# A graph layer on one core: fourteen superblocks of 128 sorted lists and 1344 gathered tiles, in place of fifteen superblocks of 125 lists and 1250 gathered tiles

## The chip, the core and the metric

The kernel runs on one core of a Trainium2 chip. The metric is the device time of one execution in microseconds (us); lower is better. The engines are named as in the profile: PE is TensorE, with its weight loads apart as PEld, DVE is VectorE, ACT is ScalarE, POOL is GpSimd, and SP is SyncE, which here only issues DMAs.

## The reference

There are 12500 nodes with 16 features and 400000 edges. The edges come sorted by their destination `dst`; `src` is random. Each edge has 64 attributes and one weight.

```python
h = jnp.maximum(_layernorm(x, axis=-1), 0.0)
# _L0_gnn_ref(h, edge_attr_64, edge_weight1, src, dst, W_node, W_review):
h = feat @ W_node.T
rf = review_feat @ W_review.T
m = (h[src_idx] + rf) * edge_w
rst = jax.ops.segment_sum(m, dst_idx, num_segments=N_NODES)
# the result
x = x + rst
```

The two projections are linear, so the kernel first sums raw attributes and raw `h` rows by destination, into `acc` (64 + 16 rows, and 16 more for a low half of `h`, by 12500 columns), and multiplies by the weights once at the end.

## The kernel before

**Tiles.** 128 edges make a tile, 3125 in all. A few tiles with neighbouring destinations are a group. For a group a 0/1 matrix is made per tile, of 128 edges by a window of 64 nodes that begins at the group's lowest destination (`find_hits`, L770, on DVE); ACT multiplies it by the edge weights (`weigh`, L551); PE multiplies the tile's 128 edges of values by it and sums over the group in one PSUM region (`sum_p` L1045, `sum_s` L1054); DVE adds the region to `acc` (`add_p` L791, `add_s` L799). A group has five tiles.

**Two ways to get `h[src]`.** For the first 1250 tiles (250 groups, "p") POOL gathers the rows from HBM, one indirect DMA for each tile (L493). For the other 1875 tiles (15 superblocks of 125 tiles, 375 groups, "s") the rows come from a table of `h` in SBUF, which holds an upper and a lower f16 half. The edges of a superblock are taken as 125 lists of 128, and each list is sorted by `src` before the main loop. Rank `j` of all lists then lies within a few chunks of 128 nodes, so `look_up` (L1019) finds it by matmuls: a 0/1 matrix `hot` of 128x125 (made on DVE, L707) times a run of table chunks. The ranks are handled in 16 steps of 8. A step has 8 ranks, 4 low digits and 2 halves, that is 64 matmuls, each with `WIDTH[x]` times 16 moving columns. DVE picks the right chunk with a mask (L749, L756, L763, L767). After 16 steps `turn_ranks` (L1027) transposes, ACT and DVE split the result into two f16 halves (L570, L808), and `unsort` (L1033) brings the rows back to the order of the edges with a permutation matrix `perm` from DVE (L781), one matmul for each tile. ACT copies them beside the attributes (`place_h`, L564).

**Phases.** Superblock 0 is looked up in a first phase (16 steps, each with one p group). Then a hardware loop of 14 phases looks up superblock t+1 while it unsorts and sums superblock t. In step x of a phase PE does, in this order, `look_up(t + 1, x)`, the `unsort` of the groups of step x+1, one `sum_p`, and the `sum_s` of the groups of step x. 25 groups go over the steps 1 to 15 by the list `SUMS`, so a step has one or two. A tail unsorts and sums the last superblock and the last 10 p groups. It also checks whether any list fell outside `WIDTH` (L917, L920); the number of passes over everything is 1 when none did and the reach of every group fits in the window.

**Order.** All is written out by hand; each engine runs its own list and waits on semaphores. Buffers: `RP = 8` slots for gathered groups, `RS = 5` for sorted ones, 4 for each of the selection matrices.

## Time and profile before

| | |
|---|---|
| median of 3 runs | 2637.76 us (2636.53 to 2643.74) |
| the profiled execution | 2632.39 us, its span 2630.7 us |
| until the first `look_up` | 160.4 us |
| first phase | 130.4 us |
| the 14 phases of the loop | 2232.5 us, 159.5 us each |
| tail, until the last add | 89.9 us |
| product with the weights, output | 17.5 us |

Times in the rows are microseconds unless marked ns, counted from the first instruction. "PEclk" is the granted share of TensorE's clock: 1.00 is 2.4 GHz and 0.50 is 1.2 GHz. "issue" marks idle time for which the profile names no other engine. PE pipelines its matmuls, so the time of a run of matmuls is best read from the start of one row to the start of the next.

### The profile page before, as it was taken

The page shows a single profiled execution, that of the slowest core. Times are in us where ns is not written, and L with a number is a line of the kernel's source. Part 1 is how long each engine was busy: PE and PEld are TensorE (multiplying, and loading weights), DVE is VectorE, ACT ScalarE, POOL GpSimd, SP SyncE. Part 2 cuts the span into 40 slices and gives each one's busy share as a digit, 9 for nine tenths or more (in the row PEclk, how much of TensorE's full clock was granted, in tenths as well). Part 3 has the DMA queues.
Part 4 walks back from the last instruction along what each step waited for, and adds up shares of the span by engine and source line. Part 5 has one row for each costly group of instructions (what it writes and reads, how often), then busy time and mean ns, then how long its engine had stood idle before and what let it go on. Part 6 is the DMA issues. An engine that isn't in the chain of part 4 may idle for free.

```text
span 2630.7 us, 72159 instructions
## 1 busy us (share of the span) xinstructions
PE 1966.3 (75%) x23874; PEld 1832.1 (70%) x23874; DVE 1524.6 (58%) x3239; ACT 911.5 (35%) x3561; POOL 1448.9 (55%) x1301
## 2 busy tenths in 40 slices
PE   1047788787878878787887878878788887887766
PEld 1046677777777777777776777777677777777765
DVE  6944555655555556555665656555555565656554
ACT  2011342433333333333433324333333333334343
POOL 3636665565655656556565555655556565656630
PEclk9577787787877878778887878878778787878855
DMA  3322233333323333233243323333333333333342
GB/s 112 48 60 57 63 77 70 80 75 68 82 68 72 77 74 77 65 84 78 65 90 68 78 62 84 83 67 74 68 69 85 67 81 74 77 70 79 75 64 43
DMA packets 512156, 191.30 MB, mean 73 GB/s; under 512 B 472234, under 2 KB 495359, under 8 KB 511479
## 3 DMA queue, kind: packets, MB, share of 16 engines
q1 hardware_dynamic: 469361, 173.64, 27.7%
q0 software_dynamic: 40000, 10.32, 4.1%
q8 instruction: 223, 3.65, 0.6%
q10 hardware_dynamic: 2368, 2.02, 0.3%
q14 instruction: 204, 1.67, 0.2%
HBM read 182.96 MB, written 2.89 MB: 71 GB/s over the span
## 4 chain that ended last, share of the span: by engine, by line
PE 65%; issue 22%; DVE 7%; ACT 2%; DMA 2%; another core or an unknown queue 1%; DVEq 1%; ACTq 0%; SPq 0%
PE found L1019 35%; PE seg L1054 16%; PE seg L1045 8%; PE edge_h L1033 5%; DMA big<-in_dst_dram 1%; ACT mid L551 1%; PE found L1027 1%; DVE by_rank L658 1%; DVE big L658 1%; DVE big L659 1%; DVE by_rank L659 1%; DVE perm L781 1%; DVE big L707 1%; ACT by_rank L570 1%
## 5 line engine op out<-in xcount | busy, mean ns | idle before, releaser
L493 POOL DMA_INDIRECT vals_p<-h_ext,idx_t x1250 | 1433.8, 1147 | 1094.9 <-PE seg L1045 700.6
L1019 PE MATMUL found<-table,big 128*128 128x128 f16 (+4 forms) x15360 | 1070.7, 233 | 377.5 <-issue 328.2
L1019 PEld LDWEIGHTS found<-table,big 128*128 128x128 f16 x15360 | 958.9, 111 | 473.5 <-issue 470.1
L551 ACT ACTIVATE sel_p<-hit_p,wgt_t 128x64 f32<-128x64 f16 x1250 | 325.4, 335 | 1208.6 <-issue 703.7
L1054 PE MATMUL seg<-mid 128*96 128x64 f32 x3750 | 506.0, 310 | 48.9 <-ACT mid L564 33.8
L1054 PEld LDWEIGHTS seg<-mid 128*96 128x96 f32 x3750 | 485.2, 224 | 52.0 <-issue 42.9
L551 ACT ACTIVATE mid<-mid,wgt_t 128x64 f32<-128x64 f16 x1875 | 468.2, 333 | 15.2 <-DVE mid L770 14.5
L749 DVE TENSOR_TENSOR masked<-found,mask 125x512 f32<-125x512 f32 x240 | 165.4, 689 | 518.5 <-PE found L1019 332.5
L707 DVE TENSOR_SCALAR big<-low_all,own 128x2004 f16<-128x2004 f16 x484 | 336.6, 738 | 11.8 <-DMA low_all<-low_dram 11.8
L1045 PE MATMUL seg<-sel_p,vals_p 128*80 128x64 f32 x2500 | 303.3, 282 | 36.0 <-issue 35.2
L1045 PEld LDWEIGHTS seg<-sel_p,vals_p 128*80 128x80 f32 x2500 | 272.5, 194 | 47.0 <-issue 45.2
L791 DVE SCALAR_TENSOR_TENSOR acc<-seg,count_p,acc 80x64 f32 x250 | 69.8, 279 | 336.5 <-issue 334.6
L1033 PE MATMUL edge_h<-by_rank,perm 128*128 128x32 f16 x1875 | 169.5, 241 | 65.9 <-issue 46.4
L781 DVE TENSOR_TENSOR perm<-edge_no,pos_t 128x768 f16<-128x768 f16 x375 | 193.4, 547 | 0.0
L1033 PEld LDWEIGHTS edge_h<-by_rank,perm 128*128 128x128 f16 x1875 | 132.7, 130 | 80.9 <-issue 67.7
L770 DVE TENSOR_TENSOR mid<-iota,rel_t 128x320 f16<-128x320 f32 x375 | 168.3, 480 | 0.0
L799 DVE SCALAR_TENSOR_TENSOR acc<-seg,count_s,acc 96x64 f32 x375 | 104.5, 279 | 107.8 <-issue 87.5
L564 ACT COPY mid<-edge_h 128x160 f32<-128x160 f32 x375 | 92.1, 287 | 215.4 <-PE edge_h L1033 184.7
L756 DVE COPY_PREDICATED masked<-mask,found 125x512 f32<-125x512 uint8 (+3 forms) x225 | 138.3, 615 | 39.0 <-DVE masked L749 33.8
L770 DVE TENSOR_TENSOR hit_p<-iota,rel_t 128x320 f16<-128x320 f32 x250 | 119.5, 478 | 0.0
L763 DVE TENSOR_TENSOR masked<-masked 125x256 f32<-125x256 f32 x240 | 100.6, 419 | 0.5
L570 ACT CAST by_rank<-found 128x1000 f16<-128x1000 f32 x30 | 29.8, 992 | 121.4 <-issue 58.0
(129 smaller groups left out, 440.3 us busy)
## 6 DMA issues: line engine op xcount, KB each, us to landing
low_all<-low_dram SPq DMA_DIRECT2D x120, 501.0 KB
mid<-in_edge_attr_dram SPq DMA_DIRECT2D x375, 160.0 KB
vals_p<-in_edge_attr_dram SPq DMA_DIRECT2D x250, 160.0 KB
vals_p<-h_ext,idx_t POOLq DMA_INDIRECT x1250
big<-in_src_dram SPq DMA_DIRECT2D x1, 1562.5 KB
big<-in_dst_dram SPq DMA_DIRECT2D x1, 1562.5 KB
big<-in_edge_weight_dram SPq DMA_DIRECT2D x1, 1562.5 KB
h_ext<-mid SPq DMA_DIRECT2D x2, 781.2 KB
```

The costliest lines, as they stand in the source:

```text
L493: pool.indirect_dma_start(vals_p[:, q % RP, j, R:F], None, h_ext, bass.IndirectOffsetOnAxis(ap=idx_t[:, q * J + j:q * J + j + 1], axis=0), ...
L551: last = nc.scalar.activation(sel[:, j, :], hit[:, j, :], ACT.Copy, scale=wgt_t[:, bass.ds(tile + j, 1)])
L707: return nc.vector.tensor_scalar(hot[:, k, a, :], low_all[:, k, :], own[:, a:a + 1], None, ALU.is_equal)
L749: nc.vector.tensor_tensor(masked[:], rows_of(x, 0, FOLD), masks_of(x, 0, FOLD), ALU.mult).then_inc(masked_low, 1)
L756: nc.vector.copy_predicated(masked[:, :, 0:WIDTH[x] - FOLD, :], masks_of(x, FOLD, WIDTH[x]), rows_of(x, FOLD, WIDTH[x])).then_inc(masked_i ...
L770: return nc.vector.tensor_tensor(hit, iota[:, 0:WINDOW].unsqueeze(1).to_broadcast([P, J, WINDOW]), rel_t[:, bass.ds(tile, J)].unsqueeze(2) ...
L781: nc.vector.tensor_tensor(perm[:, g % RS], edge_no[:], pos_t[:, bass.ds(u, 1), g, :].to_broadcast([P, P, J + 1]), ALU.is_equal).then_inc(p ...
L799: nc.vector.scalar_tensor_tensor(out=window, in0=seg_s(g), scalar=count_s[0:FS, 0:1], in1=window, op0=ALU.mult, op1=ALU.add).then_inc(acc_ ...
L1019: last = nc.tensor.matmul(found[x % 2][:, r * P:r * P + n], hot[:, x // 2 % 2, a, col:col + P], rows, start=(a == 0 and part == 0), stop=( ...
L1033: last = nc.tensor.matmul(edge_of(g)[:, q * 2 * H:(q + 1) * 2 * H], perm[:, g % RS, :, q], by_rank[:, :, :, g * J + q].rearrange("p i f -> ...
L1045: last = nc.tensor.matmul(seg_p(x), vals_p[:, slot, j, :], sel_p[:, x % RH, j, :], start=(j == 0), stop=(j == J - 1))
L1054: last = nc.tensor.matmul(seg_s(g), vals_s[:, g % RS, j, :], sel_s[:, g % RS, j, :], start=(j == 0), stop=(j == J - 1))
```

## The change

The lists become 128 for each superblock in place of 125, and the superblocks 14 in place of 15. The sorted edges are now the first 1792 tiles, and the gathered ones the last 1344 (11 tiles of the two sets overlap; their entries in the gathered set are switched off by a destination of -1). A sorted group has 8 tiles, a gathered one 6, and every step of a phase has exactly one of each, so `SUMS` is gone. The window is 56 nodes wide. `WIDTH` and `BACK`, which say how many chunks a step looks through and from where, have new values; the sum of the sixteen widths goes from 112 to 105. `find_hits` now works in f16, with the tiles innermost, so ACT reads `hit[:, :, j]` with a step of 6 or 8 elements where it read 64 in a row. The hit matrices have 2 slots in place of 4 or 5, and DVE waits for ACT before it writes one again; `RP` goes from 8 to 4, `RS` from 5 to 4. The last phase is taken out of the hardware loop and written out, without p hits for a later one; the tail has no p groups.

```diff
-J = 5
-WINDOW = 64
-LISTS = 125
-GATHERED = 10
-SORTED = 15
-GROUPS = LISTS // J
+WINDOW = 56
+LISTS = P
+SORTED = 14
+GROUPS = 16
+JS = LISTS // GROUPS
+JP = 6
-WIDTH = (4, 6, 7, 7, 7, 8, 8, 8, 8, 8, 8, 8, 7, 7, 6, 5)
+WIDTH = (4, 5, 6, 7, 7, 7, 8, 8, 8, 7, 8, 8, 7, 6, 5, 4)
-HOT = COLS * LISTS + 4
+HOT = COLS * LISTS
-RS = 5
-RP = 8
+RS = 4
+RP = 4
+RM = 2
-SUMS = [[]] + [list(range(25 * (x - 1) // 15, 25 * x // 15)) for x in range(1, STEPS)]
...
-        edge_no = sb("edge_no", [P, P, J + 1], F16)
+        edge_no = sb("edge_no", [P, P, JS], F16)
...
-                    for j in range(J):
+                    for j in range(JP):
                         pool.indirect_dma_start(
...
+            nc.scalar.copy(rel_half[:], rel_t[:]).then_inc(rel_halved, 1)
...
-                        last = nc.scalar.activation(sel[:, j, :], hit[:, j, :], ACT.Copy, scale=wgt_t[:, bass.ds(tile + j, 1)])
+                        last = nc.scalar.activation(sel[:, j, :], hit[:, :, j], ACT.Copy, scale=wgt_t[:, bass.ds(tile + j, 1)])
...
-                def find_hits(hit, tile):
-                    return nc.vector.tensor_tensor(hit, iota[:, 0:WINDOW].unsqueeze(1).to_broadcast([P, J, WINDOW]),
-                                                   rel_t[:, bass.ds(tile, J)].unsqueeze(2).to_broadcast([P, J, WINDOW]), ALU.is_equal)
+                def find_hits(hit, tiles, tile):
+                    return nc.vector.tensor_tensor(hit, edge_no[:, 0:WINDOW, 0:tiles],
+                                                   rel_half[:, bass.ds(tile, tiles)].unsqueeze(1).to_broadcast([P, WINDOW, tiles]), ALU.is_equal)
+                def hits_p(u, x, first=False):
+                    if not first:
+                        dve.wait_ge(sel_p_in, ps * NQ + u * STEPS + (x - RM + 1))
+                    find_hits(hit_p[:, x % RM], JP, u * (STEPS * JP) + (SORTED_TILES + x * JP)).then_inc(hit_p_in, 1)
...
                         if step:
+                            fold_four(u, x)
+                            dve.wait_ge(summed_s, ps * NSG + t * GROUPS + x + 1)
+                            dve.sem_inc(begun_dve, 1)
+                            add_p(u, x, added_t + 2 * x)
+                            fold_two(u, x)
+                        if step + 1 < STEPS:
+                            make_perm(t, step + 1)
...
+                        after(nc.vector.tensor_copy(rel_half[:], rel_t[:]))
...
                         look_up(t + 1, step)
                         if step == 0:
                             pe.wait_ge(rank_in, ps * (2 * SORTED) + t * 2 + 2)
-                        for g in groups_unsorted(step):
-                            unsort(t, g)
-                        bank_free(added_t, step, False)
-                        sum_p((t + 1) * STEPS + step, t * 2 + 2 + step // RP, step)
-                        for g in SUMS[step]:
-                            sum_s(t, g)
+                            unsort(t, 0)
+                        if step + 1 < STEPS:
+                            unsort(t, step + 1)
+
+                        if step >= 2:
+                            pe.wait_ge(acc_step, added + 2 * (step - 1))
+                        sum_p(t + 1, step)
+                        sum_s(t, step)
                     turn_ranks(t + 1)
+
+                with pe.Fori(0, SORTED - 2) as t:
+                    phase(t, pe.snap(ps * NG + t * PER_PHASE + (STEPS + 1)))
+                phase(SORTED - 2, ps * NG + ((SORTED - 2) * PER_PHASE + STEPS + 1))
```

On PE, the first rows of a phase in the loop, before: step 0 has one `unsort` of five tiles and no sum of sorted tiles, and step 1 has two. `found0` and `found1` are the two banks of `look_up`, `edge_h` those of `unsort`, and `seg` with `mid` is `sum_s`.

```order
L1019 MATMUL found0<-table,big 128x64 x64
L1080 REGISTER_ALU
L1031 ISA
L1033 MATMUL edge_h0<-by_rank,perm 128x32 x5
L1038 ISA
L1042 ISA
L1043 ISA
L1045 MATMUL seg0<-sel_p,vals_p 80x64 x5
L1019 MATMUL found1<-table,big 128x96 x64
```

The same place on PE with the change:

```order
L1025 MATMUL found0<-table,big 128x64 x64
L1079 REGISTER_ALU
L1037 ISA
L1039 MATMUL edge_h0<-by_rank,perm 128x32 x8
L1037 REGISTER_ALU
L1039 MATMUL edge_h1<-by_rank,perm 128x32 x8
L1044 ISA
L1047 ISA
L1048 REGISTER_ALU
L1050 MATMUL seg0<-sel_p,vals_p 80x56 x6
L1056 ISA
L1059 MATMUL seg0<-mid 96x56 x8
```

The `unsort` of two groups, and the first `sum_s`, now stand in step 0, ahead of the second `look_up`.

On DVE, the first rows of a phase in the loop, before; `mask` is made first, then half of a `hot` block (`big`), two `perm` and the hits of three groups (`hit_p`, `mid`):

```order
L732 TENSOR_TENSOR mask<-digit_now,digit 125x1024
L723 ISA
L707 TENSOR_SCALAR big<-low_all,own 128x2004 x2
L781 ISA
L781 TENSOR_TENSOR perm<-edge_no,pos_t 128x768
```

The same place on DVE with the change:

```order
L741 TENSOR_TENSOR mask<-digit_now,digit 128x1024
L732 ISA
L716 TENSOR_SCALAR big<-low_all,own 128x2048 x2
L795 ISA
L795 TENSOR_TENSOR perm<-edge_no,pos_t 128x1024
L786 ISA
L779 ISA
L779 TENSOR_TENSOR hit_p<-edge_no,rel_half 128x336
```

There is now one `perm`, of eight tiles; it is the one of group 1, which PE's second `unsort` of step 0 takes.

## Rows read from the trace of the kernel before

**Rows 1.** The page: busy time, share of the span, instructions of each engine
```profile
PE 1966.3 (75%) x23874; PEld 1832.1 (70%) x23874; DVE 1524.6 (58%) x3239; ACT 911.5 (35%) x3561; POOL 1448.9 (55%) x1301
```

**Rows 2.** Stages: length; busy of PE, PEld, DVE, ACT, POOL; PEclk, DMA share, GB/s
```profile
160.39:290.77 130.38, 93.55 (x1201) 82.84 (x1201) 63.25 (x133) 26.48 (x97) 77.45 (x75) 0.81 0.26 58
290.77:2523.26 2232.49, 1780.17 (x22050) 1668.31 (x22051) 1285.83 (x2872) 815.64 (x3248) 1291.08 (x1126) 0.81 0.33 74
2523.26:2613.20 89.94, 65.24 (x477) 62.72 (x477) 46.44 (x111) 43.85 (x185) 15.73 (x10) 0.50 0.32 49
```

**Rows 3.** Groups of PE in the loop (290.77 to 2523.26): busy, mean ns, idle before
```profile
L1054 PE MATMUL seg<-mid 128*96 128x64 f32 x3500 | 462.9, 305 | 31.6 <-ACT mid L564 17.2 <-issue 14.2
L1033 PE MATMUL edge_h<-by_rank,perm 128*128 128x32 f16 x1750 | 158.6, 240 | 54.3 <-issue 46.4 <-DVE perm L781 5.4 <-DVE by_rank L808 2.1
L1019 PE MATMUL found<-table,big 128*128 128x64 f16 x896 | 39.3, 210 | 36.6 <-DVE by_rank L808 27.0 <-issue 9.3
```

**Rows 4.** Timeline of PE at full clock, two stretches
```profile
2204.85 2.23 PE L1019 MATMUL found<-table,big 128*128 128x64 f16 x64 [1.42 <-DVE by_rank L808]
...
2481.91 0.90 PE L1045 MATMUL seg<-sel_p,vals_p 128*80 128x64 f32 x10
2482.64 1.86 PE L1054 MATMUL seg<-mid 128*96 128x64 f32 x20
2484.34 2.87 PE L1019 MATMUL found<-table,big 128*128 128x112 f16 x55
2487.41 0.26 PE L1019 MATMUL found<-table,big 128*128 128x112 f16 x2 [0.20 <-issue]
2488.19 0.21 PE L1019 MATMUL found<-table,big 128*128 128x112 f16 x1 [0.52 <-issue]
```

**Rows 5.** Timeline of PE at half clock: first phase, and the tail
```profile
160.39 3.59 PE L1019 MATMUL found<-table,big 128*128 128x64 f16 x64 [18.44 <-DVE table L813]
163.80 1.58 PE L1045 MATMUL seg<-sel_p,vals_p 128*80 128x64 f32 x10
...
173.39 5.48 PE L1019 MATMUL found<-table,big 128*128 128x112 f16 x57 [1.07 <-issue]
...
2591.22 3.43 PE L1054 MATMUL seg<-mid 128*96 128x64 f32 x20 [2.41 <-ACT mid L564]
2594.44 0.50 PE L1033 MATMUL edge_h<-by_rank,perm 128*128 128x32 f16 x5
2594.76 3.43 PE L1054 MATMUL seg<-mid 128*96 128x64 f32 x20
```

**Rows 6.** Clock of stretches within rows 4 and 5: PE busy (x), PEclk, DMA share, GB/s
```profile
2482.70:2484.40 1.70, 1.70 (x24) 1.00 0.06 11
...
173.50:178.80 5.30, 5.30 (x58) 0.50 0.17 34
```

**Rows 7.** Queues of one phase (1250 to 1410): packets, MB, share
```profile
q8 instruction: 16, 0.26, 0.7%
```

**Rows 8.** Groups of DVE and ACT in the loop, as in rows 3
```profile
L781 DVE TENSOR_TENSOR perm<-edge_no,pos_t 128x768 f16<-128x768 f16 x351 | 181.1, 547 | 0.0
L770 DVE TENSOR_TENSOR mid<-iota,rel_t 128x320 f16<-128x320 f32 x350 | 157.1, 480 | 0.0
L551 ACT ACTIVATE mid<-mid,wgt_t 128x64 f32<-128x64 f16 x1750 | 437.0, 332 | 0.7
```

**Rows 9.** Group of POOL over the span, as in rows 3
```profile
L493 POOL DMA_INDIRECT vals_p<-h_ext,idx_t x1250 | 1433.8, 1147 | 1094.9 <-PE seg L1045 700.6 <-issue 313.8 <-ACT rel_t L511 41.0
```

**Rows 10.** Timeline of PE, and of DVE, at the start of a phase
```profile
1254.28 1.59 PE L1045 MATMUL seg<-sel_p,vals_p 128*80 128x64 f32 x10
...
1256.61 1.52 DVE L707 TENSOR_SCALAR big<-low_all,own 128x2004 f16<-128x2004 f16 x2
1258.05 1.01 DVE L781 TENSOR_TENSOR perm<-edge_no,pos_t 128x768 f16<-128x768 f16 x2
```

**Rows 11.** A group of DVE in the prologue, as in rows 3
```profile
L658 DVE TENSOR_TENSOR by_rank<-big 125x960 f32<-125x960 f32 x14 | 16.9, 1207 | 0.5
```

More of the change, by code:

```diff
@@ L56 @@
 COLS = 2 * RANKS
-HOT = COLS * LISTS + 4
+HOT = COLS * LISTS
 SCALE = 8192.0
 ROUNDER = float(3 << 22)
-RS = 5
-RP = 8
+RS = 4
+RP = 4
 RH = 4
-SUMS = [[]] + [list(range(25 * (x - 1) // 15, 25 * x // 15)) for x in range(1, STEPS)]
-REST = GATHERED * GROUPS - SORTED * STEPS
-PER_PHASE = STEPS + GROUPS
-def step_of(g):
-    return [y for y in range(STEPS) if g in SUMS[y]][0]
-def place_p(x, last):
-    return min(x, REST if last else x) + sum(len(SUMS[y]) for y in range(x))
-def place_s(g, last):
-    x = step_of(g)
-    return min(x + 1, REST if last else x + 1) + g
+RM = 2
+PER_PHASE = 2 * STEPS
 def bass_gnn_preln(
@@ L389, in _ @@
                              h_ext[bass.ds(roll * (SHIFT * P), NPAD), :].rearrange("(k p) f -> p k f", p=P)).then_inc(h_back, 16)
-                for q in range(RP):
-                    load_p(q, q)
+                for step in range(RP):
+                    load_p(0, step)
                 for g in range(RS):
@@ new lines, in phase @@
+                            fold_two(u, x)
+                        if step + 1 < STEPS:
+                            make_perm(t, step + 1)
+                        else:
+                            make_perm(t + 1, 0)
+                        if step:
+                            add_s(t, x, added_t + 2 * x + 1)
+                        if step + 2 < STEPS:
+                            hits_p(u, step + 2)
+                            hits_s(t, step + 2)
+                        else:
+                            if not last:
+                                hits_p(u + 1, step + 2 - STEPS)
+                            hits_s(t + 1, step + 2 - STEPS)
@@ L976, in turn_blocks @@
                 for q, tile in enumerate(tiles):
[L977 removed]
+                    rows = tile.shape[0]
+                    last = nc.tensor.transpose(turn_bank[n % 4][:, q * rows:(q + 1) * rows], tile, ident[0:rows, 0:rows])
                 last.then_inc(turned, 1)
[L980 removed]
+            pe.wait_ge(src_float, 2)
             for k, m in idx_parts:
[L982 removed]
+                turn_blocks([src_g[:, (k + q) * P:(k + q + 1) * P] for q in range(m)])
             pe.wait_ge(rel_done, 1)
@@ L1052, in sum_s @@
                     pe.wait_ge(h_placed, ps * NSG + u * GROUPS + g + 1)
-                    for j in range(J):
+                    for j in range(JS):
                         last = nc.tensor.matmul(seg_s(g), vals_s[:, g % RS, j, :], sel_s[:, g % RS, j, :],
-                                                start=(j == 0), stop=(j == J - 1))
+                                                start=(j == 0), stop=(j == JS - 1))
                     last.then_inc(summed_s, 1)
-                def bank_free(before, x, last):
-                    if x >= 2:
-                        added = (place_s(SUMS[x - 2][-1], last) if SUMS[x - 2] else place_p(x - 2, last)) + 1
-                        pe.wait_ge(acc_step, before + added)
                 pe.wait_ge(pass_open, ps + 1)
@@ L1069, in _, with phase @@
                         pe.wait_ge(acc_step, ps * NG + (1 + step - 1))
-                    sum_p(step, step // RP, step)
+                    sum_p(0, step)
                 turn_ranks(0)
-                with pe.Fori(0, SORTED - 1) as t:
-                    added_t = pe.snap(ps * NG + t * PER_PHASE + (STEPS + 1))
+                def phase(t, added):
                     for step in range(STEPS):
```

473 lines of the change are left out of this document (232 added, 241 removed).

## The prediction

> **What bounds the kernel now.** I read the page's busy times first. PE is busy for 75% of the span, DVE 58%, POOL 55%, ACT 35% [rows 1]; no engine is full, so the shares alone decide nothing. Then the stages. The loop of 14 phases is 2232.5 of the 2630.7 us, 159.5 us a phase. In it PE is busy for 1780.2 us, the next engines for 1291.1 (POOL) and 1285.8 (DVE), and the granted clock is 0.81, so PE runs at full clock for some 60% of the time and at half clock for the rest [rows 2]. PE is idle for 2232.5 - 1780.2 = 452 us of the loop, 32.3 a phase. In the groups of PE, the waits that name another engine are 17.2 (ACT's `place_h`), 27.0 and 2.1 (the split of the ranks) and 5.4 (`perm`), together 51.7 us or 3.7 a phase. The rest, 28.6 us a phase, is "issue" [rows 3]. The timeline shows what that is: in the midst of one `look_up`, whose matmuls wait for nothing new, PE stops for about 0.5 us again and again, with one or two matmuls between the stops [rows 4]. The instruction queue q8 moves 16 packets in a phase [rows 7], and a phase has 1575 matmuls, so one packet goes with 98 of them; 28.6 / 16 = 1.8 us of stop to a packet. I read this as PE running out of instructions. So a phase is the time of PE's own matmuls, plus a toll that goes with their number, plus little else. What matters is how many phases there are, and what a phase costs PE.
>
> **What a matmul costs.** The granted clock of a stretch says which level a row belongs to [rows 6]. `look_up` by the length of its rows, half clock: 64 of 64 columns in 3.59 us, 56 ns each; 57 of 112 columns in 5.48 us, 96 ns [rows 5]. That is 13.3 ns for each unit of `WIDTH` (16 columns). Full clock: 64 of 64 columns in 2.23 us, 35 ns; 55 of 112 columns in 2.87 us, 52 ns [rows 4], 5.8 ns a unit. So `look_up` pays for its columns. The others from the start of one row to the start of the next. `sum_p` (two records a tile): 10 in 0.73 us at full clock, where the row itself is 0.90 long; at half clock the row is 1.58, so about 1.4. `sum_s`: 20 in 1.70 and in 3.22 us. `unsort`: 5 in 0.32 us, 64 ns each, at half clock [rows 4, 5]. The sums cost 73 and 85 ns a record with 80 and 96 weight columns over the same 64 moving columns, a ratio like 80 to 96 (140 and 161 at half clock). They pay for weight columns, so I give the window of 56 nothing on PE.
>
> **The change on PE, for one phase.** `look_up`: 7 units fewer, 64 matmuls each, 448 x 5.8 = -2.6 us at full clock, -6.0 at half. `sum_p`: 96 tiles for 80, 32 records more: +2.3, +4.4. `sum_s`: 128 tiles for 125, 6 more: +0.5, +1.0. `unsort`: 3 more: +0.2. Together +0.4 at full clock and -0.4 at half: nothing. The matmuls go from 1575 to 1616, so the toll grows by 2.6% of 28.6: +0.7 us. Bounds: 0, if the smaller number of waits (32 groups unsorted and summed for 50) saves as many instructions, and +1.8, one packet more.
>
> *The start of a phase.* Two `unsort`s now stand in step 0, and the second wants `perm` of group 1, which DVE makes after `mask` and half a `hot` block. In the trace DVE's `hot` pair of step 0 ends at 1258.1 [rows 10]; one wider `perm` (0.55 us for 768, some 0.7 for 1024 [rows 8]) makes 1258.8. PE was free at 1254.3 and did `sum_p` and `look_up` of step 1 before it needed a new `perm`. Now three more matmuls of the first `unsort` take it to 1254.5, and it waits some 4.3 us in step 0. Against this stand `sum_s` of group 0, which no longer waits for `place_h` later (17.2 + 5.4 us named in the loop, 1.6 a phase), and the instructions that can arrive meanwhile. Between 0 and +4.3 I take +1.
>
> *The weights of `unsort`* are read with a step of 8 elements where it was 6, since `perm` holds 8 tiles side by side. No row shows step 8. At the lower bound the cost stays 64 ns a matmul; `look_up`, with weights in a row and twice the moving columns, takes 56 ns at half clock [rows 5], so the step does seem to cost something. For the upper bound I take double, 64 x 128 = +8.2 us a phase. The nearest row is `unsort` itself, so 0. The Trainium skill, "SBUF — State Buffer", section "Door 1: The DMA port swizzle", says that SBUF has lines of 16 bytes and that each access which goes to a new line pays. By that rule steps of 6 elements (12 bytes) touch a new line three times in four and steps of 8 every time, 64 x 4/3 = 85 ns, and the whole time would be some 38 us above mine (an estimate; the 64 ns against 56 agrees in direction).
>
> Phase: 159.5 + 0 + 0.7 + 1 + 0 = 161.2 us. There are 13: 2096 us.
>
> **The other engines in a phase.** DVE drops from 41 hit matrices of 0.48 us to 32. They are all f16 now, as `perm` is, and 768 elements of that take 547 ns where 320 with an f32 input take 480 [rows 8]; so about 0.3 to 0.4 us each, 11 us for 20. `perm` 11 for 14, nine adds fewer. DVE gets about 10% lighter and was not the bound: a gain of 0 in the loop. ACT: 224 activations for 205 at 250 ns (437.0 / 1750 [rows 8]) is 56 of 161 us. Even at double the cost for the step in its input ACT stays under PE, at 112. DVE's new waits for ACT are for work of two steps ago: nothing. POOL: busy time and issue gaps make (1433.8 + 313.8) / 1250 = 1.40 us a gather [rows 9], 8.4 a step for six, against 161.2 / 16 = 10.1. With four slots a gather group is asked for three steps, 30 us, before its sum. Hidden; without that cover each step would be POOL's 8.4 us or more.
>
> **First phase.** 130.4 us [rows 2], the same for the mix of clocks. PE: `look_up` -2.6 or -6.0, `sum_p` +2.3 or +4.4: -0.3 to -1.6, I take 129.8. A step is 8.1 us there, less than POOL's 8.4, but four groups are ready and the 12 others end 12 x 8.4 = 101 us after the first sum (at about 165), before PE is at the last step (282). Hidden.
>
> **Prologue.** 160.4 us. On the path is DVE: 56 min/max operations of 960 elements, one group of 14 at 1.2 us [rows 11], now 896 elements; at 1.1 ns an element, about 70 ns less each, -3.9 us. Nine operations over all keys lose 128 elements each, -1.2. Against it four operations over `dst` grow from 3200 to 3584 elements, +1.7, and `edge_no` +0.3. Makes 157.3. ACT's `rel_half` cast falls into its wait for the sort.
>
> **Tail.** 89.9 us at half clock [rows 2]. Now 16 even steps without `sum_p`: 16 x 161 + 8 x 64 ns = 3.1 us of PE, 49.5 in all. ACT needs 8 x 0.25 us [rows 8] and a copy of some 0.4, 2.4 a step, and stays behind PE. PE was idle for 89.9 - 65.2 = 24.7 us of the tail [rows 2]: waits for `place_h` in steps with two groups (2.41 us in one [rows 5]), which go, and DVE's check of the lists and its bookkeeping for a next pass, which stay. I take half, 12.5: 62 us. With all of it the tail is 74, at full clock near 50.
>
> **Sum.** 157.3 + 129.8 + 2096 + 62 + 17.5 = 2462.6 us of span, 168 under 2630.7. The profiled execution took 1.7 more than its span, so 2464.3; the median of the runs shown was 2637.76 / 2632.39 = 1.002 of it. **2469 us**.
>
> **Rivals.**
> - *Phases get shorter too (0.17).* The even steps and the lighter DVE take away the 3.7 us of named waits, and the stops fall where PE waits anyway. For it: PE still waits for others at the start of phases. Against: 28.6 of 32.3 us are not such waits. At 154 us a phase: 2469 - 13 x 7 = 2378.
> - *The step of 8 costs PE (0.14).* If the cost goes with the length of the step, 64 x 8 / 6 = 85 ns, 14 x 2.7 us, 2507; at double, 14 x 8.2 us, 2584. For it, the slow `unsort` rows; against, that nothing here shows the weights, and not a fixed cost, to make them slow. The page named above would have the lower of the two.
> - *POOL becomes the bound (0.05).* It does from 161 / 96 = 1.68 us a gather on, against 1.40 now; at 1.75 the phase is 168 us, 2469 + 13 x 6.8 = 2557. For it, the smaller ring and more f16 operations on DVE; against, 20% of room.
> - *Slower than before (0.04).* The granted clock. By the costs above the matmuls of a phase take 97 us at full clock and 172 at half (112 units at 5.8 or 13.3 ns with 12 or 3 ns on top of each `look_up` matmul, the sums and `unsort` as above, 2 or 3 us for `turn_ranks`). The 127.2 us now (1780.2 / 14) mean that 40% of this work is done at half clock. If the new wait of 4 us at each start keeps the clock low afterwards, so that 60% is, a phase gains 15 us and stands at 176: 2469 + 13 x 15 = 2664. From 57% on it is slower. Against: PE stops in each phase now, and the clock came back each time.
> - *The change needs more than one pass (under 0.01).* Worked out from the drawn inputs, the widest group reaches 51 nodes in a window of 56 and no list falls outside the new `WIDTH`; so one pass. Two would be near 4900 us.
>
> **Range.** The forecast has 0.60; its own terms (a phase of 158 to 164, tail 50 to 75) give 2416 to 2518. With the lower half of the second rival and the upper half of the first the range is **2390 to 2550**. 0.3% is about what a measurement of this kernel can tell from no change, so: faster 0.95, within it 0.01, slower 0.04.
>
> **What would show it.** 13 phases of 159 to 163 us; PE idle about 32 us in each, most of it issue, in bursts about 100 matmuls apart; `unsort` matmuls 64 ns apart; a wait of PE for `perm` of about 4 us in step 0 of each phase; hit matrices of 0.3 to 0.4 us; POOL gathers waiting for `sum_p`; a tail near 62 us. It is wrong if the clock in the loop is off 0.81 by more than 0.03, if the idle time of PE in a phase is not tied to the number of matmuls, or if the gathers end a wait of PE.

## The result, and the profile after

The changed kernel takes 3094.4 us (median of 4 runs, 3092.8 to 3100.2), the kernel before 2637.2 us on the same chip. The ratio is 1.173, 95% interval 1.171 to 1.176: 17% slower, where 2469 us and a gain of 6% were predicted. The profiled execution took 3092.84 us, its span is 3090.9.

The stages, with the columns of [rows 2]: prologue up to 155.60, then the first phase, the twelve looped phases, the last phase (written out behind the loop), and the tail.
```profile
155.60:298.20 142.60, 90.81 (x1064) 78.78 (x1063) 54.09 (x120) 29.61 (x102) 85.17 (x87) 0.76 0.23 53
298.20:2822.00 2523.80, 1905.02 (x19393) 1813.54 (x19393) 960.47 (x2124) 844.68 (x2904) 1107.40 (x1155) 0.65 0.27 60
2822.00:2996.60 174.60, 141.25 (x1616) 134.39 (x1616) 78.39 (x177) 68.34 (x231) 73.65 (x73) 0.72 0.30 68
2996.60:3081.40 84.80, 60.72 (x442) 52.76 (x442) 37.75 (x78) 37.53 (x128) 0.00 (x0) 0.52 0.25 46
```
A looped phase lasts 2523.8 / 12 = 210.3 us, where 161.2 was predicted and 159.5 is the value of before. Its 50.8 us more have two parts. PE is idle for (2523.8 - 1905.0) / 12 = 51.6 us of it, 32.3 before: 19.3 us. PE's busy time is 158.8 us, 127.2 before: 31.6 us. The matmuls themselves did not grow, since at one clock level each costs what it did (`sum_s` 16 in 2.56 us at half clock, from 1385.89 to 1388.45 below, 160 ns each, 161 before); it is the level. With the prediction's 97 us at full and 172 at half clock, 158.8 means (158.8 - 97) / 75 = 82% of the work at half clock, 40% before. The granted clock is 0.65 where it was 0.81.

The page's busy times, and the groups of PE and POOL over the span (busy, mean ns of one, idle before them and what ended it):
```profile
PE 2226.8 (72%) x22779; PEld 2105.2 (68%) x22779; DVE 1250.6 (40%) x2627; ACT 1014.7 (33%) x3421; POOL 1327.9 (43%) x1394
...
L487 POOL DMA_INDIRECT vals_p<-h_ext,idx_t x1344 | 1314.7, 978 | 1641.8 <-PE seg L1050 1252.3
L1025 PE MATMUL found<-table,big 128*128 128x112 f16 (+4 forms) x14336 | 1196.0, 259 | 676.6 <-issue 657.7
```
The same group of `look_up` in the kernel before, over its span:
```profile
L1019 PE MATMUL found<-table,big 128*128 128x128 f16 (+4 forms) x15360 | 1070.7, 233 | 377.5 <-issue 328.2 <-DVE by_rank L808 27.0 <-DVE table L813 18.4
```
Inside the look-ups the idle time that no wait explains has doubled, 328.2 to 657.7 us, over fewer matmuls. POOL, which makes the gathers, has slack: it waits 1252.3 us for `sum_p` to free a buffer.

Where in a step this happens is seen in PE's timeline, and in POOL's of the same stretch:
```profile
1384.27 1.83 PE L1050 MATMUL seg<-sel_p,vals_p 128*80 128x56 f32 x12
1385.89 2.77 PE L1059 MATMUL seg<-mid 128*96 128x56 f32 x16
1388.45 4.00 PE L1025 MATMUL found<-table,big 128*128 128x112 f16 x46
1392.66 0.21 PE L1025 MATMUL found<-table,big 128*128 128x112 f16 x1 [0.21 <-issue]
1394.08 0.21 PE L1025 MATMUL found<-table,big 128*128 128x112 f16 x1 [1.21 <-issue]
1395.50 1.65 PE L1025 MATMUL found<-table,big 128*128 128x112 f16 x16 [1.21 <-issue]
1396.95 0.67 PE L1039 MATMUL edge_h<-by_rank,perm 128*128 128x32 f16 x8
1397.44 1.82 PE L1050 MATMUL seg<-sel_p,vals_p 128*80 128x56 f32 x12
```
```profile
1386.91 0.94 POOL L487 DMA_INDIRECT vals_p<-h_ext,idx_t  x1 [5.80 <-PE seg L1050]
...
1391.92 0.94 POOL L487 DMA_INDIRECT vals_p<-h_ext,idx_t  x1 [0.30 <-issue]
1393.17 0.94 POOL L487 DMA_INDIRECT vals_p<-h_ext,idx_t  x1 [0.30 <-issue]
1400.07 0.99 POOL L487 DMA_INDIRECT vals_p<-h_ext,idx_t  x1 [5.96 <-PE seg L1050]
```
Nearly every step is like this one. The end of `sum_p` frees a buffer, POOL makes the six gathers for it one behind another, from 1386.9 to 1394.1, and by the fifth PE stops in the look-up, comes back for one matmul, stops again for 1.2 us, and runs on at 1395.5, 1.4 us after the last gather has ended. The windows show the clock of this cycle (columns as in the stages):
```profile
1384.00:1391.00 7.00, 7.00 (x64) 7.00 (x62) 4.04 (x9) 0.37 (x1) 3.18 (x4) 0.50 0.47 114
1393.00:1395.00 2.00, 0.21 (x1) 0.19 (x2) 0.00 (x0) 2.00 (x8) 0.94 (x1) 1.00 0.09 8
1396.00:1401.00 5.00, 5.00 (x46) 5.00 (x43) 2.91 (x5) 0.37 (x1) 0.93 (x1) 0.50 0.07 17
```
In this step full clock is granted while PE stands still, half clock (1.2 GHz) when it works again.

The written-out last phase shows the rest. Its last four steps have no gathers to make for later ones: POOL's last begins at 2969.4. PE's timeline there:
```profile
2971.33 0.55 PE L1039 MATMUL edge_h<-by_rank,perm 128*128 128x32 f16 x6 [0.51 <-issue]
2971.83 1.60 PE L1050 MATMUL seg<-sel_p,vals_p 128*80 128x56 f32 x12
...
2975.79 4.38 PE L1025 MATMUL found<-table,big 128*128 128x96 f16 x64
2980.00 0.66 PE L1039 MATMUL edge_h<-by_rank,perm 128*128 128x32 f16 x8
2980.48 1.04 PE L1050 MATMUL seg<-sel_p,vals_p 128*80 128x56 f32 x12
2981.36 1.52 PE L1059 MATMUL seg<-mid 128*96 128x56 f32 x16
2982.72 2.46 PE L1025 MATMUL found<-table,big 128*128 128x80 f16 x64
2985.01 0.66 PE L1039 MATMUL edge_h<-by_rank,perm 128*128 128x32 f16 x8
```
The last stop of this kind is at 2971. The look-ups behind it run through all 64 matmuls, and from `sum_p` at 2980.5 to the end of the phase they do so at full clock. The step shown takes 2985.01 - 2980.00 = 5.0 us, where a looped one takes 13.2 on average; it is one of the narrow ones (80 columns for 64 to 128), so only a part of that is the stop and the clock.

### The profile page after: what moved, and what is told of

Same layout as the page of the kernel before. It is cut to its first block, busy times and chain, and to the rows that moved or that the text cites. A ratio compares the mean times of both kernels' runs of the same rounds, so it can differ in the third digit from the quotient of the medians.

```text
span 3090.9 us, 65695 instructions
## 1 busy us (share of the span) xinstructions
PE 2226.8 (72%) x22779; PEld 2105.2 (68%) x22779; DVE 1250.6 (40%) x2627; ACT 1014.7 (33%) x3421; POOL 1327.9 (43%) x1394
## 4 chain that ended last, share of the span: by engine, by line
PE 66%; issue 25%; DVE 5%; another core or an unknown queue 1%; ACT 1%; DMA 1%; DVEq 0%; ACTq 0%; SPq 0%
PE found L1025 35%; PE seg L1059 16%; PE seg L1050 10%; PE edge_h L1039 3%; DMA mid<-in_src_dram 1%; DVE big L716 1%; DVE big L664 0%; DVE by_rank L664 0%; DVE perm L795 0%; DVE by_rank L665 0%; DVE big L665 0%; ACT mid L547 0%; ACT by_rank L566 0%; PE found L1033 0%
## 5 line engine op out<-in xcount | busy, mean ns | idle before, releaser
L487 POOL DMA_INDIRECT vals_p<-h_ext,idx_t x1344 | 1314.7, 978 | 1641.8 <-PE seg L1050 1252.3
L1025 PE MATMUL found<-table,big 128*128 128x112 f16 (+4 forms) x14336 | 1196.0, 259 | 676.6 <-issue 657.7
L1025 PEld LDWEIGHTS found<-table,big 128*128 128x128 f16 x14336 | 1075.5, 128 | 784.7 <-issue 782.6
L547 ACT ACTIVATE sel_p<-hit_p,wgt_t 128x56 f32<-128x56 f16 x1344 | 371.5, 355 | 1351.9 <-issue 679.5
L758 DVE TENSOR_TENSOR masked<-found,mask 128x512 f32<-128x512 f32 x224 | 154.7, 691 | 1105.1 <-PE found L1025 1038.4
L1059 PE MATMUL seg<-mid 128*96 128x56 f32 x3584 | 586.3, 353 | 0.5 <-issue 0.5
L547 ACT ACTIVATE mid<-mid,wgt_t 128x56 f32<-128x56 f16 x1792 | 526.7, 376 | 36.6 <-DVE mid L779 36.6
L1050 PE MATMUL seg<-sel_p,vals_p 128*80 128x56 f32 x2688 | 385.1, 327 | 3.9 <-issue 3.9
L716 DVE TENSOR_SCALAR big<-low_all,own 128x2048 f16<-128x2048 f16 x452 | 317.0, 743 | 8.5 <-DMA low_all<-low_dram 8.5
L795 DVE TENSOR_TENSOR perm<-edge_no,pos_t 128x1024 f16<-128x1024 f16 x224 | 152.5, 681 | 0.0
L566 ACT CAST by_rank<-found 128x1024 f16<-128x1024 f32 x28 | 28.2, 1012 | 124.1 <-issue 50.6
```

The costliest lines, as they stand in the source:

```text
L487: pool.indirect_dma_start(vals_p[:, q % RP, j, R:F], None, h_ext, bass.IndirectOffsetOnAxis(ap=idx_t[:, q * JP + j:q * JP + j + 1], axis=0 ...
L547: last = nc.scalar.activation(sel[:, j, :], hit[:, :, j], ACT.Copy, scale=wgt_t[:, bass.ds(tile + j, 1)])
L716: return nc.vector.tensor_scalar(hot[:, k, a, :], low_all[:, k, :], own[:, a:a + 1], None, ALU.is_equal)
L758: nc.vector.tensor_tensor(masked[:], rows_of(x, 0, FOLD), masks_of(x, 0, FOLD), ALU.mult).then_inc(masked_low, 1)
L795: nc.vector.tensor_tensor(perm[:, g % RS], edge_no[:], pos_t[:, bass.ds(u, 1), g, :].to_broadcast([P, P, JS]), ALU.is_equal).then_inc(perm ...
L1025: last = nc.tensor.matmul(found[x % 2][:, r * P:r * P + n], hot[:, x // 2 % 2, a, col:col + P], rows, start=(a == 0 and part == 0), stop=( ...
```

## The experiments

They ran on chips of two kinds, and no number below can be read without this. The first four ran on one where the kernel before took 2586 us (kind A; the chip of the result is of this kind, with 2637). All others ran on four chips on which the same kernel took 1953 to 1965 us (kind B). Each is compared with the kernel before on its own chip. With most of the gathers left out or replaced, the changed kernel takes the same time on both kinds, as will be seen.

### Is it where TensorE's instructions stand?
The prediction put the stops down to blocks of instructions. A step is now 100 matmuls, and 1616 of them go with 16 blocks, so the fetch could hit each step at the same place. Transposes ahead of the loop move everything behind them.
```
             pe.wait_ge(placed, TURNS)
+            for _ in range(60):        # 25 in the second
+                nc.tensor.transpose(seg[0][:, 0:P], ident[:], ident[:])
```


> The changed kernel with 60 more TensorE transposes (of the identity, results unused) once, ahead of the loop over passes; they cost 3 to 8 us once. Nothing in a phase is changed, only the address at which TensorE's instructions stand. Theory A (a place-locked fetch): a step is 100 matmuls, the block of instructions that TensorE fetches is 98.5, so the fetch falls at the same place of every step, some 50 matmuls into the look-up; with the program moved by 60 matmuls it falls among the sums, where matmuls last 66 to 160 ns instead of 49 to 107 and where more of it lies beside work. Then phases go from 210 us to 155 to 190 us: 2450 to 2850 us in all, and the stalls stand 40 matmuls elsewhere in the step. Theory B (the stall belongs to the place in the work: a burst of loads and gathers behind the sums, or a wait that the trace doesn't name): the stalls stay some 50 matmuls into the look-up and the time is 3095 to 3105 us. Theory C (the work at half clock is the loss, and the stalls are only as many as before): the place moves, the time stays within 2% of 3094.

> The changed kernel with 25 more TensorE transposes once, ahead of the loop over passes (1 to 3 us). Theory A: the stalls move by about 25 matmuls within the look-up, stay in it, and phases stay between 195 and 215 us: 2900 to 3150 us. Theory B: nothing moves, 3094 to 3100 us. Theory C: moves, and 3094 within 2%.

Measured on kind A: 3016.7 us with 60 (ratio to before 1.166, 1.156 to 1.175), 3008.6 with 25 (1.162, 1.151 to 1.174); the changed kernel's own ratio, on the chip of the result, is 1.173. PE's timeline with 60:
```profile
1163.26 2.77 PE L1061 MATMUL seg<-mid 128*96 128x56 f32 x16
1165.82 3.80 PE L1027 MATMUL found<-table,big 128*128 128x112 f16 x46
1169.93 0.21 PE L1027 MATMUL found<-table,big 128*128 128x112 f16 x1 [0.30 <-issue]
1171.36 0.21 PE L1027 MATMUL found<-table,big 128*128 128x112 f16 x1 [1.22 <-issue]
```
The program moved by 60 matmuls, and the stop is again 46 matmuls into the look-up. So it is over the whole trace: the first stop of a look-up comes after 46 matmuls in the changed kernel (the median of 216 look-ups), after 47 with 60 transposes and after 47 with 25. Theory A falls: the stops are not tied to the place where an instruction stands. That does not yet say that PE has its instructions when it stops.

### Loads or gathers?
```
-                    for j in range(JP):                        # one_gather; the wait on h_in goes with it
+                    for j in range(JP if q < RP else 1):
...
-                sp.dma_start(vals_s[:, g % RS, :, 0:R], ...)   # small_loads; vals_p alike
+                sp.dma_start(vals_s[:, g % RS, 0:n, 0:R], ...) # n is 1 behind the first use
```


> The changed kernel, but after the first use of each buffer a load of edge attributes brings only one tile, not six or eight: the rest of the attributes is left out. TensorE's work is the same. Theory A: stalls at the same places, 3094 us within 2%. Theory B (the burst of loads behind the sums slows the instruction fetch): the stall of each step falls from 2.9 us to 1 to 2 us, phases of 150 to 190 us, 2350 to 2800 us.

> The changed kernel, but after the first use of each of the four buffers only one of the six gathers of a step is made: five sixths of the gathered rows are left out, and old rows are summed in their place. TensorE's work is the same. Theory A: stalls at the same places, 3094 us within 2%. Theory B (traffic of gathers behind the sums slows TensorE's instruction fetch): the 2.9 us of stall in each step fall to 1 to 2 us, phases of 150 to 190 us, 2350 to 2800 us.

Kind A: with small loads 2994.1 us (1.157, 1.149 to 1.165), within 1% of the two shifted kernels on the same chip, so next to nothing. With one gather 1635.3 us, 0.632 of before (0.627 to 0.636). Its queues, groups and the window of its looped phases:
```profile
q8 instruction: 207, 3.39, 0.9%
...
L1025 PE MATMUL found<-table,big 128*128 128x112 f16 (+4 forms) x14336 | 727.6, 214 | 82.6 <-issue 34.7
...
L487 POOL DMA_INDIRECT vals_p<-h_ext,idx_t x244 | 287.6, 1179 | 1210.4 <-PE seg L1050 1155.5
```
```profile
212.80:1435.90 1223.10, 1151.46 (x19392) 1144.63 (x19392) 953.63 (x2125) 834.72 (x2904) 211.67 (x192) 0.96 0.50 118
```
The instruction queue q8 moves as many packets as ever, 207 for 210, at twice the rate, and 34.7 us of unexplained idle time are left of 657.7. The clock is 0.96, a phase 1223.1 / 12 = 101.9 us. Theory B holds for the gathers and not for the loads, and far more strongly than its 2350 to 2800 us. This is the run that shows the cause: on a chip of the kind of the result, the gathers bring both the stops and the low clock. The Trainium skill, "Runtime: NRT & Kernel Launch", section "Instruction fetch mechanics", says that the fetch of the next block is mostly hidden. This trace agrees: 34.7 us over 207 packets is at most 0.17 us each.

### What of a gather does it, and how many?
```
-                    for j in range(JP):
+                    for j in range(JP if q < RP else 3):     # three_gathers; 5 in five_gathers
...
+                        if q >= RP and j:                    # plain_dma; pool_fill has a memset of 1200 bytes a row here
+                            pool.dma_start(vals_p[:, q % RP, j, R:F], h_ext[0:P, :]).then_inc(h_in[q % RP], 16)
+                            continue
...
+                        if q >= RP and j == 2 and q - RP >= STEPS:     # spread
+                            pool.wait_ge(summed_s, ps * NSG + (q - RP - STEPS + 1))
...
+                        if q >= RP and j == 4:
+                            pool.wait_ge(found_in, ps * NQ + (q - RP + 2))
```


> The changed kernel with three of the six gathers of a step (after the first use of each buffer); the other rows are left out. With all six a phase is 210 us (203 on the chip of the last runs) with 45 us of stall in its look-ups, with one it is 98 to 101 us with none. Theory D (a slowed supply of TensorE's instructions: the gathers slow it in proportion to their number): stall of 15 to 25 us in a phase, phases of 125 to 160 us, 2000 to 2450 us. Theory E (a threshold: only a burst of gathers that still runs some 45 matmuls into the look-up, 6 us after the sums began, meets TensorE at full clock there): three gathers end within 3.8 us, stalls vanish, phases of 98 to 105 us, 1620 to 1700 us.

> The changed kernel with one gather of six, and in the place of each other gather a plain transfer of the first 128 rows of h_ext, the same 8 KB into the same place and from the same engine's queue (the gathered rows are left out). Theory G (the traffic of small transfers and their semaphore updates stalls TensorE): stalls as with six gathers, 2700 to 3100 us. Theory H (it is the indirect form, whose descriptors the chip has to make at run time): no stall, 1620 to 1750 us.

> The changed kernel with one gather of six, and in the place of each other gather a memset of about 1 us by POOL (five sixths of the gathered rows are left out). Theory F (POOL being busy, or its port into SBUF, is what stalls TensorE): the stalls come back, 2700 to 3100 us. Theories D and E (the gathers' transfers and what they need do it, not POOL's time): as with one gather and idle POOL, 1600 to 1700 us.

> The changed kernel with all its work; of a group's six gathers the third and fourth wait until the next sum of sorted tiles is done, the fifth and sixth until the next look-up is done, so that no burst is longer than two. Theory E (a burst that reaches into the look-up): the look-up holds at most two gathers in its first 2.5 us, stalls of under 15 us in a phase, 1700 to 2300 us. Theory D (the number of gathers): little changes, 2850 to 3050 us. A wait of a sum for gathers that come too late would show as idle time before the sums released by POOL's transfers, and isn't expected, since they are needed three steps later.

The memset run also waits for the end of each memset. All four ran on kind B, where before took 1960.7 us: three gathers 1637.0 us, plain transfers 1637.5, memsets 2166.6 (1.105, 1.102 to 1.109), which neither theory had, spread 2006.1 (1.024, 1.019 to 1.028). The values could not be laid beside the 3010 us of kind A, so the changed kernel itself was run on kind B.

> The changed kernel as it is, beside the kernel before and the next three on one chip, since the kernel before took 2586 us on the chip of the first four experiments and 1961 us on that of the second four. If the ratio to before is a matter of the program alone it is 1.17 again. If the stall of TensorE's look-ups is what differs from chip to chip, both kernels move with the chip, and on a chip where before takes 1961 us the changed one takes 1950 to 2100 us.

> All the work, each group's six gathers in three pairs (the second pair behind the sum of sorted tiles, the third behind the next look-up), now beside the changed kernel on the same chip. Theory E (the unbroken burst of six gathers is what starves TensorE): clearly under the changed kernel, by 10% or more on a chip on which that is slow (before at 2586 us). Theory D (their number): within 3% of the changed kernel.

> The changed kernel with five of the six gathers of a step (the other rows left out), as many as the kernel before makes at each sum. If the sixth gather in a burst is what made the change slow: 2300 to 2650 us on a chip with before at 2586 us. If the stall needs only more than three: within 5% of the changed kernel.

> The kernel before with one of the five gathers of a group after the first use of each of its eight buffers (the other rows left out). It says what the kernel before would take if gathers cost TensorE nothing. If both kernels pay the same kind of toll, it falls far below before: 15 phases of about 100 us and a tail of 99, 1700 to 1800 us, over the 1635 us that the changed kernel takes with one or three gathers, so that the change is worth what I predicted or so (6%) without the toll. If the toll is new in the changed kernel, it stays within 5% of before.

The changed kernel 2011.0 us, 1.025 of before (1.018 to 1.032); spread 2013.0 (1.026); five gathers 1730.5 (0.882), which neither of its two forecasts has; the kernel before with one gather 1773.3 (0.904). Here the change costs 2.5% and not 17%, and the trace says by what. The chain that ended last, and the groups of the changed kernel on kind B:
```profile
POOL 61%; issue 20%; PE 8%; DVE 7%; DMA 3%; ACT 1%; POOLq 0%; DVEq 0%; SPq 0%; ACTq 0%
...
L488 POOL DMA_INDIRECT vals_p<-h_ext,idx_t x1344 | 1405.7, 1046 | 490.1 <-issue 428.4
L1026 PE MATMUL found<-table,big 128*128 128x112 f16 (+4 forms) x14336 | 800.0, 223 | 57.2 <-issue 24.8
...
L1051 PE MATMUL seg<-sel_p,vals_p 128*80 128x56 f32 x2688 | 269.9, 258 | 212.5 <-DMA vals_p<-h_ext,idx_t 210.1
```
```profile
250.40:1790.10 1539.70, 1321.64 (x19394) 1306.76 (x19394) 966.78 (x2124) 834.99 (x2905) 1188.04 (x1154) 0.85 0.45 99
```
There is next to no stop inside the look-ups (24.8 us). POOL no longer waits for PE; it gathers all the time, (1405.7 + 428.4) / 1344 = 1.36 us a gather over the span and 1539.7 / 1152 = 1.34 in the loop, 16 x 6 x 1.34 = 128.3 us for a phase. PE waits 210 us for gathered rows at `sum_p`. Shown once in PE's timeline:
```profile
1002.35 0.71 PE L1040 MATMUL edge_h<-by_rank,perm 128*128 128x32 f16 x8
1004.71 1.82 PE L1051 MATMUL seg<-sel_p,vals_p 128*80 128x56 f32 x12 [1.65 <-DMA vals_p<-h_ext,idx_t]
```
The other runs on this kind fit. With five gathers POOL and PE are nearly even: 80 x 1.36 = 109 us of gathers, where the window of the twelve phases has 107.9, and PE waits 66 us for gathered rows:
```profile
235.10:1529.90 1294.80, 1194.92 (x19393) 1186.06 (x19394) 970.46 (x2125) 835.96 (x2905) 1000.98 (x965) 0.93 0.52 116
```
With three (65 us a phase), PE binds, at 1637 us, where one gather took 1635 on kind A. Memsets of 1.19 us, 1.32 with the waits between them, bring the bound back, although only one row in six is gathered, and the look-ups have no stops (26.6 us). So here it is POOL's time, as the rival in the prediction had it. Plain transfers, of the same bytes in the same number of packets, take 0.57 us of POOL each and cost the kernel nothing:
```profile
q0 software_dynamic: 43008, 11.10, 5.5%
...
L488 POOL DMA_DIRECT2D vals_p<-h_ext x1100 | 597.5, 571 | 13.0 <-issue 12.9
```
Spreading a burst can't help an engine that is never idle. None of these runs says what of a gather stops PE on kind A: the forecasts of no stop that came true here, with three gathers and with plain transfers, prove nothing, since on kind B even six gathers bring none. The Trainium skill, "Perfetto Trace Analysis", section "DMA Instruction — SWDGE (GPSIMD)", says that the profile ends such an instruction when its last descriptor is written, not when data have moved. The 0.94 us of a gather are then POOL's own work, and the trace agrees: POOL's time is the bound while its queue q0 takes 5.8% of the transfer engines.

Three of these were run once more, again on kind B, so that what they were to tell of kind A stays untold:

> The changed kernel with five of six gathers in a step. Of the kernels so far, the changed one took 2011 us beside a before of 1963 us, with a phase of 128 us = 96 gathers at 1.33 us and no stall inside the look-ups; on other chips it took 3010 to 3094 us beside 2586 to 2637 us, with stalls of 45 us in the look-ups of a phase. This run is for a chip of the second kind: if the toll on TensorE goes by the number of gathers, 2650 to 2850 us; if the sixth in a row brings it from the level of before, 2300 to 2500 us. On a chip of the first kind 1730 us again.

> The changed kernel with three of six gathers in a step. On a chip with before at 2586 us or more: by number 2200 to 2400 us, by burst (a threshold between three and five) 1630 to 1800 us. On a chip with before at 1960 us: 1637 us again.

> All the work, the six gathers of a group in three pairs. On a chip with before at 2586 us or more: if the unbroken burst makes the stall, 2300 to 2700 us against the 3010 to 3094 us of the changed kernel; if the number does, 2900 to 3050 us. On a chip with before at 1960 us: 2010 us again, since gathers one behind another are the bound there.

> All the work, the six gathers of a group in three pairs, once more, for a chip with before at 2586 us or more: if the unbroken burst makes the stall, 2300 to 2700 us; if the number does, 2900 to 3050 us. On a chip with before at 1960 us: 2010 us as twice before.

1730.3, 1641.9, 2012.9 and 2009.4 us, the earlier values to 0.3%.

### Fewer gathers for more phases
```
-SORTED = 14                +SORTED = 16
-JP = 6                     +JP = 5
-                    for j in range(JP):
+                    for j in range(0 if RP <= q < STEPS else JP):
```


> All the work with fewer gathers: 16 sorted superblocks (2048 tiles) and 16 x 16 groups of five gathered tiles, of which the first 203 tiles repeat sorted ones and count for nothing; in the first phase, which holds only such tiles, the gathers behind the first four groups are left out. 1220 gathers in place of 1344, two phases more, a phase of 104 to 106 us where gathers are the bound. On a chip with before at 1960 us: 15 looped phases of 106, first phase 62 to 70, prologue 155, tail 100: 1900 to 1960 us. On a chip with before at 2586 us or more, phases of 150 to 160 us as before has with its five: 2550 to 2750 us.

It took 21507 us, eleven times its forecast: two superblocks more bring sorted lists that reach below the starts of ranks 73 to 77, and the kernel goes round twelve times. With the table one unit wider in the tenth step:
```
-WIDTH = (4, 5, 6, 7, 7, 7, 8, 8, 8, 7, 8, ...      BACK[9] = 13.25
+WIDTH = (4, 5, 6, 7, 7, 7, 8, 8, 8, 8, 8, ...      BACK[9] = 15.75
```


> The kernel with 16 sorted superblocks again, with the table one unit wider in the tenth step (8 units for 7, 64 more columns in 64 matmuls), since in the two superblocks more some sorted lists reach one block of 128 nodes below the start of ranks 73 to 77, which sent the last run into a second loop of passes: its 21507 us are twelve passes, (21507 - 175) / 12 = 1778 us each. One pass: 1778 + 175 + 5 for the wider step = 1950 to 1965 us on a chip with before at 1957 us, the same as before. On a chip with before at 2586 us or more: 2550 to 2750 us if five gathers in a burst cost what they cost in before.

1931.7 us on kind B, all the work done, a little under its forecast of 1950 to 1965: 0.986 of before (0.984 to 0.988), and by the ratios to before 4% under the changed kernel. Its group of POOL:
```profile
L487 POOL DMA_INDIRECT vals_p<-h_ext,idx_t x1220 | 1285.0, 1053 | 526.4 <-issue 364.2
```
1220 gathers at 1.35 us are 1649 us, and the kernel is 1932; the changed kernel's 1344 were 1834 of 2011. It wasn't run on kind A.

## Why the prediction was wrong

**The step that failed** is what the toll goes with: "28.6 / 16 = 1.8 us of stop to a packet. I read this as PE running out of instructions", and so "a toll that goes with their number", +0.7 us for 2.6% more matmuls. It grew by 19.3 us a phase, and took the clock down with it, 31.6 us more. The stops do not move with the instructions and are gone when gathers are left out; they go with the bursts of gathers. That holds for the kernel before too. In its records PE has 429 us of stops longer than 0.25 us, of any cause, that begin between 300 and 2500 us. Each set against the first gather of the burst it falls in, 369 of the 429 us begin 3 to 7 us behind that; in the changed kernel 488 of 536 begin 4 to 9 us behind it. That is 429 / 217 bursts of five = 2.0 us a burst before, 536 / 168 bursts of six = 3.2 after. The numbers 16 packets and 16 bursts in a phase were alike by chance, and I took the first without asking for the second. A step still has one burst after the change, and its toll is 1.6 times as long. That the one gather more does this, and not the smaller ring of buffers or the new order, is argued and not shown.

The records say one thing more. Counted from the first gather of a burst, the first stop of the changed kernel comes after 49 to 59 matmuls in eight bursts of ten, although 3.1 to 6.1 us pass by then; and the last stop ends 1.2 to 1.4 us after the last gather in as many, whatever PE is at. So the toll of a burst is its length and 1.3 us, less the time that PE needs for some 55 matmuls: about (7.2 + 1.35) - 5.2 = 3.4 us for six gathers, at the medians. That looks as if PE lived on instructions it had in hand while the gathers hold up the next ones. The prediction would then be right in that PE runs out of instructions, and wrong in what makes it. It would not be by a slower transfer of instructions: a packet of q8 takes 1.08 us with all gathers and 1.06 us with one in six (medians). No run shows the supply inside PE, so this stays a reading. In the kernel before it is looser: 44 to 67 matmuls.

**What the gathers cost in all.** With most of them left out the kernels take 1773 us (before, one gather of five, kind B) and 1635 us (changed, one of six, kind A; on kind B 1637 with three, and 1637 with one and five plain transfers). So the work that I costed did shrink, by 138 us of the 168 forecast. The times with all gathers on the chip of the result are 864 us above the first, for 968 gathers left out, 0.89 us each, and 1459 us above the second, for 1100, 1.33 us each. The 864 us take one number from each kind of chip, as the kernel before with one gather was not run on kind A. On kind B it is 1963 - 1773 = 190 us and 2011 - 1637 = 374 us. The change makes 96 gathers in a phase for 80, and I had looked only at whether POOL finishes in time.

**The clock.** The rival "slower by the granted clock" had the place of the loss, more than 57% of the work at half clock, and its 2664 us are 430 short: 82% was. Its cause was another. The wait for `perm` in step 0 is there, 28.2 us in the twelve phases, 2.35 each and 4.24 at most; here it is 1.13 us behind a first stop of 2.47,
```profile
1140.16 3.33 PE L1025 MATMUL found<-table,big 128*128 128x64 f16 x59 [2.47 <-issue]
1143.30 0.66 PE L1039 MATMUL edge_h<-by_rank,perm 128*128 128x32 f16 x8
1145.09 0.69 PE L1039 MATMUL edge_h<-by_rank,perm 128*128 128x32 f16 x8 [1.13 <-DVE perm L795]
```
and it is in one step of sixteen, where nearly each step has its stop. By time, 62% of a phase's loss (31.6 of 50.8 us) is the clock and 38% the stops. The clock is low behind other pauses of PE too: the tail has no gather, PE pauses 1.15 us for `perm` in most of its steps, and the granted clock is 0.52, where from 2980 to 2990 us, without a pause, it is 1.00. Whether it would have stayed up with the same stops at other places was not tried.

**The rival POOL** named what binds on kind B, not what made the change slow on the chip of the result. It was dismissed by a wrong comparison: 1.40 us a gather against 161 / 96 = 1.68. Those 161 us held the toll of the gathers themselves. Against PE's phase without it, 101.9 us, POOL binds from 1.06 us on.

**Right:** the prologue (155.6 for 157.3); `unsort`, whose step of 8 costs nothing (8 from 1396.95 to 1397.44 above, 61 ns each, 64 before, so the 85 ns and 128 ns of its rival did not come); the window of 56, which gives PE nothing; matmul work unchanged (96 us a phase with one gather, at a clock of 0.96, where the prediction has 97 at full clock); hits of 0.33 and 0.38 us; one pass; 13 phases behind the first. **Wrong in size:** the first phase, 142.6 for 129.8, by the same stops; the tail, 84.8 for 62. There each step takes 4.4 us and not 3.1, since DVE makes a step's `perm` only behind the add of the sum before, which waits for PE, and so PE waits 1.15 us for it. Of the tail's 24.7 us of idle time the prediction kept half, and 84.8 - 60.7 = 24.1 stayed, 8.06 of them in one wait behind the check of the lists and its bookkeeping (5.25 before):
```profile
3045.26 0.70 PE L1039 MATMUL edge_h<-by_rank,perm 128*128 128x32 f16 x8 [1.15 <-DVE perm L795]
3045.79 2.78 PE L1059 MATMUL seg<-mid 128*96 128x56 f32 x16
3049.72 0.70 PE L1039 MATMUL edge_h<-by_rank,perm 128*128 128x32 f16 x8 [1.15 <-DVE perm L795]
```

Two of the prediction's own signs of being wrong came: the clock in the loop is 0.65 and not within 0.03 of 0.81, and PE's idle time is not tied to the number of matmuls.

**Open.** Why a burst of gathers stops PE on chips of kind A, and not on B, where POOL gathers without a pause; what of a gather does it there, POOL's time, the indirect form or the transfer, since the runs that tell these apart were all on kind B; whether the toll there goes by the length of a burst, by the gathers in a phase, or by the four buffers in place of eight; and what sixteen superblocks would give there.

## What to carry to other kernels

Idle time that a profile calls "issue" has no cause yet. Before a toll is tied to a count, ask which other things happen as often: here packets of instructions and bursts of gathers both came 16 times a phase. Leave one of them out and look. One run would have settled this, and would also have shown that the gathers, made by an engine that is 55% busy and has slack, were worth some 860 us. An experiment meant for one chip has to be compared on that kind of chip: the runs that should have split the cause further ran on chips where the effect is absent. And to judge whether an engine has room, set it against the bound engine's time without the stalls that it may itself cause.

## What the runs showed of the hardware

- The same program took 2637, 2586 and 1961 us on different chips, each within 0.5% of itself, while the changed kernel took 1635 us with one gather of six on kind A and 1637 us with three of six on kind B. What differs is what gathers do to TensorE: 657.7 us of unexplained idle time in the look-ups on the one kind, 24.8 on the other.
- In the stop at 1392 TensorE's instructions come one by one: a matmul at 1392.66, a weight load at 1393.38, a matmul at 1394.08, a weight load at 1394.80, a matmul at 1395.50, 0.7 us apart each, with ACT at work all along.
```profile
1393.38 0.10 PEld L1025 LDWEIGHTS found<-table,big 128*128 128x128 f16 x1 [1.04 <-issue]
...
1394.80 0.10 PEld L1025 LDWEIGHTS found<-table,big 128*128 128x128 f16 x1 [1.32 <-issue]
```
- A gather of 128 rows of 64 bytes holds POOL for 1.25 to 1.40 us (in the kernels with all gathers 0.98 to 1.15 on average, 0.94 for many of them, and 0.30 between two). A plain transfer of the same 8 KB takes 0.57 us of POOL: replacing 1100 of 1344 removed the bound.
- The stops end 1.2 to 1.4 us after the last gather of a burst of six, in eight of ten bursts of the changed kernel on kind A.
